# Low-digit one-hots made by ScalarE from the score sums instead of by VectorE from the digits

## The reference

```python
user_emb = table_user[user[:, 0]]
item_emb = jnp.concatenate([table_i1[item[:, 0]], table_i2[item[:, 1]], table_i3[item[:, 2]]], axis=1)
ub = jnp.concatenate([table_i1[rec_his[:, :, 0]], table_i2[rec_his[:, :, 1]], table_i3[rec_his[:, :, 2]]], axis=2)
mask = rec_his[:, :, 0] == 0
q = jnp.broadcast_to(item_emb[:, None, :], ub.shape)
att_in = jnp.concatenate([q, ub, q - ub, q * ub], axis=-1)
h = att_in @ w_att1.T + b_att1
score = (h @ w_att2.T + b_att2)[..., 0]
score = jnp.where(mask, 0.0, score)
browse = jnp.einsum('bl,ble->be', score, ub)
feat = jnp.concatenate([item_emb, browse, user_emb], axis=-1)
x = _dice(feat @ w1.T + b1, a1, g1, be1)
x = _dice(x @ w2.T + b2, a2, g2, be2)
x = jax.nn.sigmoid(x @ w3.T + b3)
```

## Time and profile before

| what | value |
|---|---|
| median of 3 runs | 1508.28 us (1501.13 to 1511.05) |
| profiled execution, span | 1506.3 us (the page names no other time of that execution) |
| PE busy | 1299.2 us, 86% |
| DVE busy | 1405.9 us, 93% |
| ACT busy | 758.1 us, 50% |
| POOL busy | 1188.4 us, 79% |
| `scale`, L1038 | 256 of 2105 ns |
| `pick`, L1026 | 512 of 772 ns |
| `onehot_high`, L994 | 256 of 1157 ns |
| `onehot_low`, L1012 | 256 of 829 ns |

### The profile page before, as it was taken

One profiled execution on the slowest core, in us unless ns is written; L12 is line 12 of the kernel. 1 busy time (PEld: TensorE's weight loads), 2 busy tenths in 40 slices (PEclk: granted clock), 3 DMA queues, 4 the chain that ended last, 5 costly groups with the idle time before them and its releaser, 6 DMA issues.

```text
span 1506.3 us, 66273 instructions
## 1 busy us (share of the span) xinstructions
PE 1299.2 (86%) x27007; PEld 1186.0 (79%) x27007; DVE 1405.9 (93%) x1397; ACT 758.1 (50%) x1729; POOL 1188.4 (79%) x1671
## 2 busy tenths in 40 slices
PE   5688989889898988889898998989899898988864
PEld 4577878888887988788788888878888887888761
DVE  6699999999999999899999999999999999999945
ACT  5554455555445555454555554454555545452217
POOL 3588788888888888788888888888888888888830
PEclk8899999999999999999999999999999999999966
DMA  3566676666667666666766666666676666565820
GB/s 51 111 137 127 127 143 133 141 144 141 124 137 143 130 146 140 127 133 133 143 131 142 146 141 134 130 137 132 143 143 140 141 132 138 131 149 133 153 54 1
DMA packets 517508, 194.38 MB, mean 129 GB/s; under 512 B 485445, under 2 KB 493237, under 8 KB 517245
## 3 DMA queue, kind: packets, MB, share of 16 engines
q1 hardware_dynamic: 499654, 162.61, 53.5%
q10 hardware_dynamic: 15448, 26.51, 6.7%
q0 software_dynamic: 2144, 1.36, 0.8%
HBM read 8.45 MB, written 1.44 MB: 7 GB/s over the span
## 4 chain that ended last, share of the span: by engine, by line
POOL 72%; issue 15%; PE 3%; DVE 3%; POOLq 3%; ACT 2%; DMA 1%; ACTq 1%; SPq 0%; DVEq 0%
POOL score L439 24%; POOL score_r L448 14%; POOL score L444 11%; POOL parts L449 9%; POOL parts L452 6%; POOL item_rows L417 4%; POOL parts L445 3%; POOL user_rows L425 2%; DVE score_j L1026 1%; DVE onehot_lo L1012 1%; ACT scores_b L775 1%; PE sel L727 1%; DMA hiT<-onehot_hi 1%; POOLq L437 1%; POOLq L443 1%
## 5 line engine op out<-in xcount | busy, mean ns | idle before, releaser
L560 PE MATMUL wsum_ps<-scaled_lo,onehot_hi 100*128 100x75 bf16 x12288 | 535.0, 201 | 81.5 <-DVE scaled_lo L1038 80.2
L543 PEld LDWEIGHTS sel<-scoretab,hiT 128*128 128x128 bf16 x12288 | 495.8, 99 | 121.6 <-DMA hiT<-onehot_hi 59.2
L543 PE MATMUL sel<-scoretab,hiT 128*128 128x75 bf16 x12288 | 534.5, 201 | 63.1 <-DMA hiT<-onehot_hi 43.9
L1038 DVE TENSOR_TENSOR scaled_lo<-onehot_lo,parts 100x3744 bf16<-100x3744 bf16 x256 | 539.0, 2105 | 34.4 <-POOL parts L452 26.4
L560 PEld LDWEIGHTS wsum_ps<-scaled_lo,onehot_hi 100*128 100x128 bf16 x12288 | 486.1, 99 | 106.3 <-DVE scaled_lo L1038 101.7
L439 POOL TENSOR_TENSOR score<-score_j 100x16 f32<-100x16 f32 x256 | 386.6, 1510 | 156.6 <-DVE score_j L1026 155.7
L768 ACT ACTIVATE wsum_ring<-wsum_ps 128x300 f32<-128x300 f32 x512 | 215.5, 421 | 525.7 <-PE wsum_ps L560 497.2
L1026 DVE TENSOR_REDUCE score_j<-sel 100x24 f32<-100x600 f32 x512 | 395.5, 772 | 21.0 <-PE sel L543 21.0
L994 DVE TENSOR_TENSOR onehot_hi<-digits,iota_hi 100x1920 bf16<-100x1920 bf16 x256 | 296.1, 1157 | 3.4 <-PE wsum_ps L560 3.3
L775 ACT ACTIVATE scores_b<-acc 128x512 bf16<-128x512 f32 (+1 forms) x318 | 255.4, 803 | 50.0 <-issue 22.7
L448 POOL TENSOR_TENSOR score_r<-score,parts 100x16 f32<-100x16 f32 x256 | 207.3, 810 | 20.0
(11 more groups left out here) (168 smaller groups left out, 724.0 us busy)
## 6 DMA issues: line engine op xcount, KB each, us to landing
scoretab<-scores_b SPq DMA_DIRECT2D x384, 93.8 KB
weightsum<-wsum_ring ACTq DMA_DIRECT2D x128, 125.0 KB
weightsum<-wsum_ring ACTq DMA_DIRECT2D x64, 150.0 KB
raw<-in_r_rec_his_dram SPq DMA_DIRECT2D x32, 150.0 KB
hiT<-onehot_hi SPq DMA_TRANSPOSE x256, 3.8
x_rows<-x_tile SPq DMA_DIRECT2D x14, 100.0 KB
scores_b<-x_rows SPq DMA_DIRECT2D x1, 1400.0 KB
item_rows<-in_L_rec_table_i_dram,ids_now POOLq DMA_INDIRECT x51
```

Of the source, the lines that this page charges most:

```text
L543: mm = pe.matmul(sel[:, 2 * (s % 2) + q, (c % 4) * W:(c % 4 + 1) * W] .rearrange("p (j v) -> p j v", j=NF), hiT[0:HJ, s // 2 % 4, g * POSP ...
L560: mm = pe.matmul(wsum_ps[:, s % 2, b * W:(b + 1) * W].rearrange("p (j v) -> p j v", j=NF), hi_columns(ring_slot(n), g), scaled_lo[:, n % 2 ...
L1038: ins = dve.tensor_tensor(scaled_lo[:, n % 2, :, :, :].rearrange("p q i (u d) -> p (q i) u d", d=2), onehot_lo[:, n % 2, :, :, :].rearrang ...
```

## The change

- `onehot_low` moves from VectorE's step to ScalarE's slot and is cut in two halves, one per slot. It no longer compares digits with a row of numbers. It reads the same `sel` banks as the reduce and computes Relu(1 + 2 x sel / 2^100), which is 1 in the column of the low digit and 0 elsewhere. It is the first thing that ScalarE does in a slot, and waits for the reduce of that slot (`score_ready`).
- TensorE's read block of slot s waits for that activation of slot s-2 as well (`lo_ready`, k-1).
- `onehot_lo` has 75 + 1 columns for a half history in place of 3 x 26, so the scale handles 3648 elements in place of 3744.
- The low digits are no longer kept in `digits`. Once a half tile, two activations of 384 elements write the digit less the centre and its square into `low_rows`, and `lo_rows` becomes one copy of 96 elements a step in place of two activations of 48.

```diff
@@ pe, read_scores @@
                 if not (isinstance(k, int) and k < 2):
                     pe.wait_ge(score_ready, k - 1)
+                    pe.wait_ge(lo_ready, k - 1)
@@ act, task "digit" @@
-                            act.wait_ge(lo_ready, (t - 1) * STEPS + 8 * hb + 8)
...
+                            act.wait_ge(lo_rows_ready, (t - 1) * STEPS + 8 * hb + 8)
...
+                    if kind == 1:
+                        ins = act.activation(digits[:, hb, :, :, :].rearrange("p g j d -> p j g d"),
+                                             src.unsqueeze(3).to_broadcast([POS, NF, 2 * HALF, 2]), ACT.Copy)
+                    else:
+                        rows = low_rows[:, hb, :, :, :].rearrange("p g j i -> p j g i")
+                        act.activation(rows[:, :, :, 0], src, ACT.Identity, bias=centre[:, :])
+                        ins = act.activation(rows[:, :, :, 1], src, ACT.Square, bias=centre[:, :])
@@ act @@
+            def onehot_low(t, s):
+
+                k = t * SLOTS + s
+                n, g0 = s // 2, (s % 2) * 8
+                act.wait_ge(score_ready, k + 1)
+                if s % 2 == 0 and not (isinstance(k, int) and k < 4):
+                    act.wait_ge(scaled_ready, t * STEPS + n - 1)
+                act.activation(onehot_lo[:, n % 2, g0:g0 + 8, 0:W].rearrange("p (q c) u -> p q c u", q=2),
+                               sel[0:POS, 2 * (s % 2):2 * (s % 2) + 2, 0:4 * W].rearrange("p q (c u) -> p q c u", u=W),
+                               ACT.Relu, bias=one[:, :], scale=2.0 / FAR).then_inc(lo_ready, 1)
@@ act, lo_rows @@
-                act.activation(rows[:, :, :, 0], low, ACT.Identity, bias=centre[:, :])
-                act.activation(rows[:, :, :, 1], low, ACT.Square, bias=centre[:, :]).then_inc(lo_rows_ready, 1)
+                act.activation(onehot_hi[0:POS, ring_slot(n), :, 1:1 + 2 * NF],
+                               low_rows[:, hb, g0:g0 + PER, :, :].rearrange("p g j i -> p g (j i)"), ACT.Copy
+                               ).then_inc(lo_rows_ready, 1)
@@ act, slot @@
             def slot(t, s, odd, last=False):
                 here = tasks_of(t)
+                onehot_low(t, s)
@@ dve @@
-            def onehot_low(t, n):
...
-                if not (isinstance(k, int) and k < 2):
-                    dve.wait_ge(scaled_ready, k - 1)
-                dve.tensor_tensor(onehot_lo[:, n % 2, :, :, :].rearrange("p q j (v d) -> p (q j) v d", d=2),
-                                  digits[:, hb, 0, g0:g0 + PER, :, :].rearrange("p g j d -> p (g j) d").unsqueeze(2)
-                                  .to_broadcast([POS, PER * NF, LP // 2, 2]),
...
-                                  ALU.is_equal).then_inc(lo_ready, 1)
@@ dve, scale @@
-                dve.wait_ge(lo_ready, k + 1)
+                dve.wait_ge(lo_ready, 2 * k + 2)
@@ dve, step @@
-                onehot_low(t, n)
```

More of the change, by code:

```diff
@@ L36, in build @@
     LP = LO + 1
-    HJ, U, W = HB + NF * HI, NF * LP, NF * LO
+    HJ, W = HB + NF * HI, NF * LO
+    U = W + 1
     TILE, HALF = 128, 64
@@ L69, in build @@
         onehot_hi = sb("onehot_hi", [POSP, RING, PER, HJ], BF16)
-        onehot_lo = sb("onehot_lo", [POS, 2, PER, NF, LP], BF16)
+        onehot_lo = sb("onehot_lo", [POS, 2, PER, U], BF16)
+        one = sb("one", [POS, 1])
         scaled_lo = sb("scaled_lo", [POS, 2, PER, 3, U], BF16)
@@ L77, in build @@
         parts = sb("parts", [POS, 2, PER, 3, 2], BF16)
-        digits = sb("digits", [POS, 2, 2, 2 * HALF, NF, 2], BF16)
+        digits = sb("digits", [POS, 2, 2 * HALF, NF, 2], BF16)
+        low_rows = sb("low_rows", [POS, 2, 2 * HALF, NF, 2], BF16)
         far_rows = sb("far_rows", [1, 3, LO], BF16)
@@ L174, in build @@
         lo_ready = sem("lo_ready")
+        lo_rim_zero = sem("lo_rim_zero")
         hiT_in = [sem(f"hiT_in{i}") for i in range(4)]
@@ L803, in task @@
                         else:
-                            act.wait_ge(lo_ready, (t - 1) * STEPS + 8 * hb + 8)
-                    src = (misc_b if kind == 1 else misc)[0:POS, 0:2 * NF * HALF]
-                    ins = act.activation(digits[:, hb, kind, :, :, :].rearrange("p g j d -> p j g d"),
-                                         src.rearrange("p (j g) -> p j g", j=NF).unsqueeze(3)
-                                         .to_broadcast([POS, NF, 2 * HALF, 2]), ACT.Copy)
+                            act.wait_ge(lo_rows_ready, (t - 1) * STEPS + 8 * hb + 8)
+                    src = ((misc_b if kind == 1 else misc)[0:POS, 0:2 * NF * HALF]
+                           .rearrange("p (j g) -> p j g", j=NF))
+                    if kind == 1:
[5 more added lines that the diff above has]
+                        ins = act.activation(rows[:, :, :, 1], src, ACT.Square, bias=centre[:, :])
                 elif name == "item":
@@ L880, in lo_rows @@
                     act.wait_ge(wsum_full, sums_before(k, n))
-                low = digits[:, hb, 0, g0:g0 + PER, :, 0]
-                rows = onehot_hi[0:POS, ring_slot(n), :, 1:1 + 2 * NF].rearrange("p g (j i) -> p g j i", i=2)
-                act.activation(rows[:, :, :, 0], low, ACT.Identity, bias=centre[:, :])
-                act.activation(rows[:, :, :, 1], low, ACT.Square, bias=centre[:, :]).then_inc(lo_rows_ready, 1)
+                act.activation(onehot_hi[0:POS, ring_slot(n), :, 1:1 + 2 * NF],
+                               low_rows[:, hb, g0:g0 + PER, :, :].rearrange("p g j i -> p g (j i)"), ACT.Copy
+                               ).then_inc(lo_rows_ready, 1)
             def slot(t, s, odd, last=False):
                 here = tasks_of(t)
+                onehot_low(t, s)
                 if s in here:
@@ L921, in slot @@
                     split_copy(r, stage, SPLIT_DONE * (t + 1) + (3 * r + stage + 1), 1 - odd)
-            act.wait_ge(bias_ready, 4)
+            act.wait_ge(bias_ready, 5)
             scale_raw(0, 0)
@@ L1039, in scale @@
                     scaled_lo[:, n % 2, :, :, :].rearrange("p q i (u d) -> p (q i) u d", d=2),
-                    onehot_lo[:, n % 2, :, :, :].rearrange("p q j v -> p q (j v)").unsqueeze(2)
+                    onehot_lo[:, n % 2, :, :].unsqueeze(2)
                     .to_broadcast([POS, PER, 3, U]).rearrange("p q i (u d) -> p q i u d", d=2),
@@ L1076, in _ @@
             dve.memset(offset[:, :], -float(MID) / LO).then_inc(bias_ready, 1)
+            dve.memset(one[:, :], 1.0).then_inc(bias_ready, 1)
             dve.memset(w2col[:, :], 0.0).then_inc(dve_tail_pre, 1)
@@ L1096, in _ @@
             dve.memset(hiT[:, :, PER * POSP:], 0.0).then_inc(dve_tail_pre, 1)
+            dve.memset(onehot_lo[:, :, :, W:U], 0.0).then_inc(lo_rim_zero, 1)
+            dve.wait_ge(lo_rim_zero, 1)
             dve.wait_ge(rim_zero, 1)
```

12 lines of the change are left out of this document (2 added, 10 removed).

## The result

The changed kernel takes **1567.5 us** (median of 4 runs, 1559.6 to 1578.2), the kernel before 1506.8 us beside it: a ratio of 1.041 with a 95% interval of 1.036 to 1.046. It is slower by 4%, where 1490 was forecast, and outside the range of 1400 to 1555. The profiled execution has a span of 1564.1 us (1506.3 before) and a mean granted clock of 0.941 (0.957 before).

The account below looks back on a forecast made before the run. VectorE was taken to set the pace, its step falling from 5.23 to 4.43 us, with a ScalarE-TensorE ring just closing. Middle tiles -3, first -5, last -9: 1506.3 - 17 = 1489, stated as 1490; range 1400 to 1555.

Parts of the forecast that it names:

- the price of the two low-digit activations: ScalarE, once a half tile: one 0.86 us digit copy becomes two of 384 elements, 0.5 each, up to 1.6 together.
- the forecast's own ring: Two-slot loop: reduce, ScalarE's activation and copies, TensorE's split piece and read block, reduce; 4.29 or 4.09 us against VectorE's 4.43.
- slots 2 to 7: Middle tile's first stretch: ring with both digit copies, three issues and an "all" piece gives 15.5 us, 0.9 gained.
- slots 20 to 25: ScalarE works without pause through digit copies, issues and split copies, then the id scaling: 17.6 us, 1.9 lost.
- the last stretch: Slots 26 to 31, 0 and 1: VectorE paces at 4.55 us a step, 19.2 of the old 21.8, 2.6 gained.
- Its list of ScalarE's transfers: DMA issues of the collected sums on ScalarE, 0.4 us each, in slots 4 to 6, 16 to 18 and 20 to 22.
- the first and last tile: First tile, without browse product or first layer: 5 us gained; last tile, without splits and hence ring: 9 gained.
- three stretches of four: Middle tile's slots 2 to 7, 8 to 19 and 20 to 25, forecast at 15.5, 34.1 and 17.6 us.
- The ring gives: Rival: ScalarE's idle time absorbs the new work, TensorE's load remains, 81.5 us a tile; 1412 us, chance 0.27.
- The ring binds: Slower rival: activation costs 1.25 us like score copies, each two-slot ring 0.46 longer; 1547 us, chance 0.25.
- GpSimd: Rival: its chain may add 0.2 us to each free step; 1506 us, counted within the forecast's own width.

Follow-up runs that it names:

- After: The changed kernel itself, as described under The change, against the kernel before: 1567.5 us, ratio 1.041.
- e1: The changed kernel with low_rows laid out so that each half-tile digit activation writes neighbouring elements: 1522.7 us, 1.010 to the kernel before.
- e4: The kernel before with only the new low_rows in the slow layout and one rows copy a step, one-hot still on VectorE: 1520.5 us, 1.008.
- e3: e1 with the low one-hot activation moved from first to last in ScalarE's slot: 1436.5 us, 0.953 to the kernel before.
- e8: e1 with the low one-hot activation over only half of the positions (output not the reference's): 1488.8 us, 0.991 to the kernel before.
- e11: e3 with the low one-hot activation over only half of the positions (output not the reference's): 1419.5 us, 0.946 to the kernel before.
- e10: e1 with the third window's transfers of sums issued in slots 1 to 3 of the next tile: 1517.4 us, 1.011 to the kernel before.

## Why the prediction was wrong

**The step that failed** is the price of the two low-digit activations, "0.5 each with the bias, 1.0 together (up to 1.6 by the score copies)". They are 3.26 us of busy time, and hold ScalarE's queue for 2.46 (701.25 to 703.70, and so in the mean), beyond its upper bound. I had the right warning in hand: score copies of 384 elements at 802 ns, "those copies write runs of three". I applied it to the large activation, which writes runs of 75 and kept its price of 760 ns, and treated it only as a bound for the small ones, whose output elements stand alone. No row of before had such a write, and a run of three isn't as bad as it gets. At the true price in the queue the forecast's own ring gets 1.5 us longer in slots 2 to 7 and in slots 20 to 25. After and e1 are 1.54 us apart in the queue, and 2.02 and 1.39 in these stretches: 3.4 for 3.1. Worth in time: 45 us of the 77 that were missing. e4 shows that the reordering isn't needed for this cost.

**The second** is the last stretch, 19.2 forecast, 21.5 in after and 22.8 in e1. The term had taken the transpose's time from one place of the run before, and answered with 9.1 us for two steps, which is the floor. Its list of ScalarE's transfers names slots 4 to 6, 16 to 18 and 20 to 22 and leaves out 28 to 30, the third window. So it left out that these and the placements fall into the same steps, and that ScalarE's issues move back with its work. In spans: e1 is 46.6 us above the forecast, 35 from the middle tiles (2.9 on each over 86.4 + 0.6, less 0.45 because the mean tile before takes 87.65 and not the 87.2 of the one I read), 4.6 and 5.8 from the first and last tile, where 5 and 9 us of gain were forecast and 0.4 and 3.2 came, and 1.3 from a longer set-up.

**What held.** VectorE's share fell to 78% ("near 80%"). Its wait for TensorE is 217 us (above 150), TensorE's for score copies 121 (50 or more), ScalarE's busy time 1043 us (1040 to 1080), the activation's mean 0.760 (0.75 to 0.82). In slots 20 to 25 the ring was the right mechanism: e1 takes 17.69 there (17.6 forecast), and opening the ring in e3 gives 15.06. With the layout mended, three stretches of four are within 0.6 us of the forecast, and their sum within 0.1, but that is in part luck. In slots 2 to 7 TensorE is idle for only 0.9 of e1's 15.89 us, e3 without the ring takes 15.56, and the shorter activation of e8 changes nothing. So TensorE's own work sets the pace there, and the 15.5 of the forecast's ring came out right for another reason.

**The rivals.** "The ring gives" (1412, 0.27) did not come, against the ring as built; e3 (1436.5) and e11 show how near it comes once the ring is open. "The ring binds" (1547, 0.25) has the right sign and nearly the right time for the wrong reason: it wanted an activation of 1.25 us. The scattered write that it feared was in another instruction. Its condition should have been stated for every new write of the change. Its own sum doesn't close either: 3.8 us a tile in one place and 4.1 in the next, which is 1542 or 1546. GpSimd never bound: VectorE waited 10 us for it.

**What stays open.** Why slot 0's wait varies between nothing and 7 us from tile to tile in after and e1 is not settled; no run changed the placements' bytes or separated their time from that of the sums' transfers. Nor is it settled why the transpose of the earlier trace rows took 5.6 us with seven transfers around it and e1's 10 with nine. And where in e3 the activation's length still costs 11 to 17 us was not traced.

## What to carry to other kernels

Work moved onto an engine with idle time is put in that engine's order, and where it stands there decides more than its price: here the same activation costs 86 us more at the head of a slot than at its end, because everything behind it inherits its wait. Price each new instruction by the layout of what it writes as well as by its count of elements, and where a row warns of a layout, try the warning on every write of the change. Where a step gets shorter, count the transfers and bytes that are issued in it, not only the latency of the one transfer that is waited for.

## What the runs showed of the hardware

- A ScalarE activation from PSUM with bf16 output takes 592 to 600 ns for 384 elements written side by side, 1573 and 1685 ns for 384 written 12 bytes apart, and 760 and 510 ns for 600 and 300 in runs of 75, that is 0.83 ns for each further element in such runs. Score copies of 384 elements in 128 runs of three and of 512 in 128 runs of four took 802 and 804 ns (kernel before). Gathering 96 elements from six separate rows cost 83 ns more than reading them in a row.
- The Trainium skill, "ScalarE: Activation LUTs", section "Rules for kernel authors", gives relu to VectorE. On the price the traces agree: 829 ns once a step on VectorE, 760 twice on ScalarE. The changed kernel is slower, as the rule would have it; e3 isn't: the same Relu on ScalarE is in a kernel 4.7% faster than the one that has the one-hot on VectorE.
- After TensorE idled for 2.06 us of four in after, and for 6.91 us in e1, the granted clock fell to 0.50, and read blocks took 1.73 and 1.70 us, not 1.01. A wait of TensorE can thus cost more than its own length. The slow blocks add up to 44 us in after, 50 in e1, 27 before and 25 in e3.
- A transpose of one step's block took 5.6 us to its reader in the kernel before, with seven other transfers issued around it, and 10 us in e1 with nine. Moving three transfers away from the tile's end (e10) brought slot 0's reduce from 11.8 to 9.1 us after slot 28's.
